# Attention over 16 heads of width 16: one block of keys in four as one full-width product, and stores waited for by halves

## The reference

```python
rx = _apply_rope(x)
q, k, v = (proj(Wq, bq), proj(Wk, bk), proj(Wv, bv))     # 16 heads of width 16
scores = jnp.einsum('bhqd,bhkd->bhqk', q, k) / np.sqrt(hd)
attn = jax.nn.softmax(scores, axis=-1)
attended = jnp.einsum('bhqk,bhkd->bhqd', attn, v)
attended = attended.transpose(0, 2, 1, 3).reshape(b, s, d)
return attended @ Wo.T + bo
```

## Time and profile before

| | us |
|---|---|
| median of 3 runs | 2109.47 (2102.84 to 2113.85) |
| the profiled execution | 2103.16 |
| its span in the profile | 2101.8 |
| TensorE busy in the span | 1683.6 (80%) |
| VectorE busy | 1234.1 (59%) |
| ScalarE busy | 1032.3 (49%) |
| POOL busy | 988.7 (47%) |

### The profile page before, as it was taken

The page is one execution under the profiler, slowest core; times in us unless marked ns, Lnnn a source line. Parts: engine busy times, 40 slices in busy tenths (PEclk is TensorE's granted clock), DMA queues, the critical chain, the costliest instruction groups (busy, mean ns, idle before and its releaser), DMA issues. The chain is left out here.

```text
span 2101.8 us, 23811 instructions
## 1 busy us (share of the span) xinstructions
PE 1683.6 (80%) x7418; PEld 1232.8 (59%) x7419; DVE 1234.1 (59%) x2317; ACT 1032.3 (49%) x1981; POOL 988.7 (47%) x824
## 2 busy tenths in 40 slices
PE   5698894999935887878882989989998998679882
PEld 2477673777723665656652656656666665556661
DVE  5655554666547685959853665575675674452224
ACT  2154442555401675757782665665675765052220
POOL 1200002243233474657770574574674676048884
PEclk9899997999965898999996999999999999669996
DMA  2300003444235222213002010120120110138776
GB/s 78 122 11 31 1 21 126 114 126 111 61 85 130 71 61 62 50 46 85 21 1 98 21 42 21 32 61 21 31 60 24 29 52 24 59 77 200 179 178 161
DMA packets 96787, 146.17 MB, mean 70 GB/s; under 512 B 22711, under 2 KB 61820, under 8 KB 93830
## 3 DMA queue, kind: packets, MB, share of 16 engines
q1 hardware_dynamic: 65104, 102.69, 16.9%
q0 software_dynamic: 18432, 26.36, 6.9%
q10 hardware_dynamic: 13126, 15.60, 2.4%
HBM read 101.83 MB, written 36.41 MB: 66 GB/s over the span
## 5 line engine op out<-in xcount | busy, mean ns | idle before, releaser
L2183 POOL TENSOR_TENSOR STp_lo_use<-ST_use,STp_hi_use 128x512 fp32r<-128x512 f32 x256 | 333.8, 1312 | 227.8 <-ACT ST_use L2032 226.7
L1712 POOL TENSOR_TENSOR STp_lo<-ST,STp_hi 128x512 fp32r<-128x512 f32 x192 | 255.8, 1349 | 141.1 <-ACT ST L1480 140.3
L2096 DVE TENSOR_REDUCE nmax_use<-bank 128x1 f32<-128x512 f32 x256 | 173.3, 679 | 114.4 <-PE bank L1940 110.0
L2028 ACT ACTIVATE STp_hi_use<-bank 128x512 fp32r<-128x512 f32 x256 | 153.0, 597 | 173.2 <-PE bank L1966 170.4
L1476 ACT ACTIVATE STp_hi<-bank 128x512 fp32r<-128x512 f32 x256 | 158.8, 620 | 82.2 <-PE bank L1414 81.5
L1601 DVE TENSOR_REDUCE nmax<-bank 128x1 f32<-128x512 f32 x256 | 168.6, 680 | 41.5 <-PE bank L1403 41.0
L1403 PE MATMUL bank<-rows_k,rows_q 65*128 65x512 f32 x256 | 125.4, 498 | 66.0 <-DVE nmax L1601 48.1
L1480 ACT ACTIVATE ST<-bank 128x512 f32<-128x512 f32 x256 | 160.0, 625 | 0.0
L2032 ACT ACTIVATE ST_use<-bank 128x512 f32<-128x512 f32 x256 | 151.8, 593 | 2.1 <-POOL STp_lo_use L2183 2.1
L1940 PE MATMUL bank<-ks,qs 128*128 128x512 f32 x256 | 112.2, 440 | 36.2 <-DVE nmax_use L2096 14.9
L918 POOL TENSOR_SCALAR veps<-mv 128x4 f32<-128x4 f32 x4 | 0.9, 228 | 249.6 <-DVE mv L867 249.6
(11 more groups left out here) (428 smaller groups left out, 4558.6 us busy)
## 6 DMA issues: line engine op xcount, KB each, us to landing
stage<-in_W SPq DMA_DIRECT2D x16, 1024.0 KB, 4.9
Wgu<-in_Wgu SPq DMA_DIRECT2D x32, 384.0 KB, 3.4
rows_q<-hop_scratch SPq DMA_DIRECT2D x32, 256.0 KB, 4.6
ks<-ks SPq DMA_DIRECT2D x64, 128.0 KB, 2.3
rinv<-rinv_scratch SPq DMA_DIRECT2D x64, 128.0 KB, 2.9
rows_k<-hop_scratch SPq DMA_DIRECT2D x24, 256.0 KB, 5.6
hop_scratch<-qkp_hi SPq DMA_DIRECT2D x20, 256.0 KB
Wda<-in_Wdn SPq DMA_DIRECT2D x32, 128.0 KB, 3.6
```

Source lines behind the costliest of these rows:

```text
L1712: G.tensor_tensor(STp[u % NHI][1], ST[u % NFULL], plain(STp[u % NHI][0]), ALU.subtract).then_inc(low["pool"].sem, low["pool"].inc(u))
L2028: A.activation(STp[u % NHI][0], bk.ap, ACT.Exp)
L2096: V.tensor_reduce(nmax[:, (h % 2) * TB + j:(h % 2) * TB + j + 1], bk.ap, AX.X, ALU.max, negate=True).then_inc(bk.free, 1)
L2183: G.tensor_tensor(STp[u % NHI][1], ST[u % NFULL], plain(STp[u % NHI][0]), ALU.subtract).then_inc(low["pool"].sem, low["pool"].inc(u))
```

## The change

One block in four, u % 4 = 3, is called whole. For it ScalarE takes the exponential once, in full, into one of two new buffers `whole_ST`; there is no subtraction; and TensorE weighs it in one full-width float32 product with the same stationary columns. The other three blocks stay as they were, all their subtractions on POOL. The pairs of `STp` become four, used by these blocks alone, and the buffers `ST` three.

SP's stores of q's and k's parts wait for the first half, issue its stores, and then wait for the second half. ScalarE, before it writes a half of `qkp`, waits for the stores of that half alone. Stores of q stand at step 30 of the program where they were at 33, stores of k at 36 where they were at 39; no other issue of SP lies between. VectorE waits for its own last division before the next one.

```diff
-    NHI, NFULL = 5, 4
+    NHI, NFULL = 4, TB - 1
+        whole_ST = [sb("whole_ST%d" % z, [P, S]) for z in range(2)]
-        low_by = [("dve" if u % 4 == 3 else "pool") for u in range(END)]
+        whole = [u % TB == TB - 1 for u in range(END)]
+        low = Signal(kit, "s4_low", [u for u in range(END) if not whole[u]])
+        def parts_of(u):
+            return STp[(u // TB * NFULL + u % TB) % NHI]
...
-                    PE.wait_ge(low[low_by[u]].sem, low[low_by[u]][u])
-                    PE.matmul(bk.ap, Vone[:, kt, h, :], STp[u % NHI][0], start=k == 0 and kt == 0, stop=False)
-                    PE.matmul(bk.ap, Vone[:, kt, h, :], STp[u % NHI][1], start=False, stop=k == HG - 1 and kt == TB - 1).then_inc(weighed.sem, weighed.inc(u))
+                    if whole[u]:
+                        PE.wait_ge(ST_BANKS[u % 2].free, ST_BANKS[u % 2].free_at["scores", u])
+                        PE.matmul(bk.ap, plain(Vone[:, kt, h, :]), whole_ST[u // TB % 2], start=False, stop=k == HG - 1).then_inc(weighed.sem, weighed.inc(u))
+                    else:
+                        PE.wait_ge(low.sem, low[u])
+                        PE.matmul(bk.ap, Vone[:, kt, h, :], parts_of(u)[0], start=k == 0 and kt == 0, stop=False)
+                        PE.matmul(bk.ap, Vone[:, kt, h, :], parts_of(u)[1], start=False, stop=False).then_inc(weighed.sem, weighed.inc(u))
...
+                    if whole[u]:
+                        if u >= 2 * TB:
+                            A.wait_ge(weighed.sem, weighed[u - 2 * TB])
+                        A.activation(whole_ST[u // TB % 2], bk.ap, ACT.Exp).then_inc(bk.free, 1)
...
-                            all_hopped(A, b if n else b - 1, 1 - n)
+                            A.wait_ge(hopped[1 - n][g].sem, hopped[1 - n][g][b if n else b - 1, len(HOPS[1 - n]) - 1])
...
-                if 0 <= u < END and low_by[u] == "dve":
-                    bk = ST_BANKS[u % 2]
-                    V.wait_ge(bk.free, bk.free_at["scores", u])
-                    if u >= NHI:
-                        V.wait_ge(weighed.sem, weighed[u - NHI])
-                    V.tensor_tensor(STp[u % NHI][1], ST[u % NFULL], plain(STp[u % NHI][0]), ALU.subtract).then_inc(low["dve"].sem, low["dve"].inc(u))
...
+                        if b or g:
+                            V.wait_ge(att_done.sem, att_done[(b, g - 1) if g else (b - 1, GROUPS - 1)])
...
-                    b = of_next(s, (33, 39)[n])
+                    b = of_next(s, (30, 36)[n])
                     if b:
-                        for g in range(DC):
-                            SP.wait_ge(stack_bank(b, n, g).free, stack_bank(b, n, g).free_at["stack", b, n, g])
                         if b > 1 and n == 0:
                             for i in range(QUARTERS):
                                 SP.wait_ge(stacked[i].sem, stacked[i][b - 2, 3])
                         for g in range(DC):
+                            SP.wait_ge(stack_bank(b, n, g).free, stack_bank(b, n, g).free_at["stack", b, n, g])
                             hop(SP, b, n, g)
```

More of the change, by code:

```diff
@@ L1282, in self_heads @@
         v_zeroed = Signal(kit, "s4_v_zeroed", ["V"])
-        low_by = [("dve" if u % 4 == 3 else "pool") for u in range(END)]
-        low = {e: Signal(kit, "s4_low_" + e, [u for u in range(END) if low_by[u] == e]) for e in ("dve", "pool")}
+        whole = [u % TB == TB - 1 for u in range(END)]
+        low = Signal(kit, "s4_low", [u for u in range(END) if not whole[u]])
         rowed = [Signal(kit, "rowed%d" % z, [(b, i) for b in range(B) for i in range(z, QUARTERS, 2)], step=16) for z in range(2)]
@@ L1310, in head_columns, with parts_free @@
             return bass.AP(Vone.tensor, Vone.offset + g * HG * P + n, [Vone.ap[0], [H1 * P, TB], [P + BLOCK, HG], [1, k]])
+        def parts_of(u):
+            return STp[(u // TB * NFULL + u % TB) % NHI]
+        def parts_free(u):
+            n = u // TB * NFULL + u % TB - NHI
+            return n // NFULL * TB + n % NFULL if n >= 0 else None
         def of_batch(s, r):
@@ L1706, in pool @@
                 u = s - ST_LAG - 1
-                if 0 <= u < END and low_by[u] == "pool":
+                if 0 <= u < END and not whole[u]:
                     bk = ST_BANKS[u % 2]
                     G.wait_ge(bk.free, bk.free_at["scores", u])
-                    if u >= NHI:
-                        G.wait_ge(weighed.sem, weighed[u - NHI])
-                    G.tensor_tensor(STp[u % NHI][1], ST[u % NFULL], plain(STp[u % NHI][0]), ALU.subtract).then_inc(low["pool"].sem, low["pool"].inc(u))
+                    before = parts_free(u)
+                    if before is not None:
+                        G.wait_ge(weighed.sem, weighed[before])
+                    G.tensor_tensor(parts_of(u)[1], ST[u % TB], plain(parts_of(u)[0]), ALU.subtract).then_inc(low.sem, low.inc(u))
                 for c in range(DC):
```

16 lines of the change are left out of this document (8 added, 8 removed).

## The result

| | before | after |
|---|---|---|
| median (range) of 4 runs each, us | 2106.15 (2102.48 to 2113.85) | 2056.74 (2050.18 to 2063.77) |
| ratio, 95% interval | | 0.976 (0.9736 to 0.9785) |
| span of the profiled execution | 2101.8 | 2048.9 |
| granted clock over the span | 0.908 | 0.915 |

The forecast was 2077 us with 2056 to 2102 as its range: right in direction, 20 us too high, and the time lies at the range's low edge.

The account below looks back on a forecast made before the run. VectorE was taken as late, in small pieces everywhere and large ones at batch boundaries. Terms -17 - 13.5 - 2 + 0 = -32.5 us; against the timed median of 2109.5 the forecast is 2077 us, range 2056 to 2102.

Parts of the forecast that it names:

- Halves: Batch boundaries: storing and waiting by halves removes ScalarE's three DMA waits and some slow clock; -17 us (-8 to -19).
- what would show it: Signs of right: no DMA wait before L1521, first-half stores within 1 us, plain stretches 35 to 37 us, VectorE under 32.
- Plain stretches: Three stretches of plain running: VectorE's subtraction goes, TensorE sets the pace; -13.5 us (-20 to -3).
- The floor of 34.4 us: Plain stretch of 32 steps: TensorE's own work after the change, 31.2 + 8 x 0.40 us.
- Price of the full-width product: TensorE, each whole block: 0.86 us against 0.46 for the fp32r pair, +0.40 us, 64 times 25.6 us.
- Boundaries: First 32 blocks of each batch: whole blocks' dearer products and removed subtractions cancel; 0 us (-8 to +8).
- 1013.8 to 1061.5 and the end: End of batch 2: -2 us, waits go; last 33 us: 0 us, POOL full before and after.
- TensorE eats the relief: Rival, plain stretches: dearer product cancels the relief, only the halves' gain remains; 2092 us, chance 0.14.
- The halves bring nothing: Rival, boundaries: ScalarE waits for stores as before, only the whole blocks' gain remains; 2094 us, chance 0.08.
- Slower: Rival: full product on the path everywhere, no relief from VectorE; +12 us, 2121 us, chance 0.05.
- The pauses take the clock with them: Rival: boundaries run at full clock and win 5 us each beyond the sum; 2060 us, chance 0.07.

Follow-up runs that it names:

- e1: Kernel before with only SP's stores and ScalarE's waits done by halves, no whole blocks; 2084.20 us, ratio 0.9899.
- e7: Changed kernel, but ScalarE again waits for the stores of both halves while SP still issues them by halves; 2067.32 us, ratio 0.9784.
- e2: Changed kernel with SP's stores and ScalarE's waits as before, so only one block in four whole; 2075.57 us, ratio 0.9857.
- e3: Kernel before without VectorE's 64 subtractions, ScalarE's second exponential written as the low part, TensorE's product pair kept; 2078.67 us, ratio 0.9876.
- e8: Changed kernel run once more, word for word, for a second trace; 2057.35 us, ratio 0.9746.
- e6: Changed kernel with two blocks in four whole instead of one, 128 full-width products; 2071.98 us, ratio 0.9823.
- e5: Changed kernel with each whole block weighed by two fp32r products (0.46 us) instead of one full-width product (0.86); 2047.58 us, ratio 0.9701.

## Why the prediction was right in direction and too small

**Halves: mechanism right, size 2.7 us short.** Forecast -17 (to -19), e1 gives -19.7 at the boundaries. No DMA wait is left before L1541, and the stores go out within 1 us, as "what would show it" asked. That the sum came so near is in part luck: its part for the clock was scaled from the second boundary to all three, and e1 took 12.2, 4.9 and 2.7 us off the three. The longest landing of a store, 7.8 us, was misread: by line, the 3.0 to 7.8 us of the earlier trace rows are those of the 20 loads (L1582), and the profile gives none for the stores (L1571). The conclusion held; the last of q's stores was issued at 807.18 us and ScalarE released by 813.89, 6.7 us later. Which of the two edits does it was not asked (e7).

**Plain stretches: right.** Forecast -13.5, measured -13.8, and -14.3 in the second trace. VectorE is under 32.1 us in each. The floor of 34.4 us was 0.6 short: the third stretch takes 35.0 with no gap. The others, at 39.2 and 39.7, took longer than the 35 to 37 that the text named; they began at 43.8 and 44.4 by this cut, so the gain was there and the level was not.

**Price of the full-width product: right.** It was taken from two rows of other shapes. TensorE's timeline in the changed kernel, the scores' product of three steps, the first step with a whole block:

```profile
944.96 0.40 PE L1425 MATMUL bank<-rows_q,rows_k 66*128 66x512 f32 x1
...
946.29 0.40 PE L1425 MATMUL bank<-rows_q,rows_k 66*128 66x512 f32 x1
...
947.23 0.40 PE L1425 MATMUL bank<-rows_q,rows_k 66*128 66x512 f32 x1
```

1.33 us against 0.94: +0.39, forecast +0.40.

**Boundaries: the step that failed.** The prediction gave the whole blocks 0 us here (between -8 and +8): "24 products add 9.6 us and up to 4 us more at the lower clock; 24 subtractions go, but a good half of them lie in time in which VectorE waits for ScalarE anyway". Measured -10.5 alone (e2). The subtractions were sized about right: the text left them some 10 to 13 us to cancel the products, and e3, which removes them alone, gives 11.0 (193.0 against 204.0). What failed is the charge on the other side, 9.6 us in full and up to 4 us more at the lower clock: with it e2 would lie 9.6 to 13.6 us above e3, and it ends at 193.5 us against 193.0. Two things stand in its place. At one and the same granted clock the price reaches the end in part: 2.1 of 3.2 us in the second boundary (64.8 us in e3 and 66.9 in e2, both at 0.92), and 5.4 to 5.9 of 9.6 us over the three, between e5 and the changed kernel. The error there was to charge TensorE's work in full at a place where it had idle time (55.22 us busy in a second boundary of 69.4), one paragraph after writing that "what counts is the place". And the clock moved the other way: instead of a surcharge at the lower level, it stands at 0.87, 0.92 and 0.92 with the whole blocks alone, where the kernel before has 0.81, 0.86 and 0.90 and e3 0.81, 0.92 and 0.88. How the rest divides between this clock and the 24 exponentials that e2 saves and e3 does not is open; no run takes the exponentials away alone.

**1013.8 to 1061.5 and the end: right.** Forecast -2 and 0; measured -0.3 and -1.6 in the first trace, -2.8 and -1.6 in the second. The last stretch takes 30.2 us where the same cut has 31.8 before; on the 33.0 of the earlier trace rows that is some 31.4, just under the 32 to 34 of the text. The Trainium skill (SBUF — State Buffer, section "SBUF: two separate sides") has the loser of the port pair that VectorE and GpSimd share blocked for a whole instruction, and by that rule the end would be 1 to 2 us shorter; the trace agrees with its POOL part (1349 to 1314 ns a subtraction; VectorE's own took 0.68 us in the median, 1.02 in the mean and 1.78 at most), but e3 shows that this alone doesn't shorten the stretch (31.6 us, ScalarE the bound): it took the saved exponential as well.

**The sum.** With the terms as e1 and e2 have them, the boundaries give -30.2 instead of -17, and the stage -45.7; measured -43.2 and -45.8. The medians differ by 49.4 us here and 53.3 beside e8. What stands between 45 and 50 to 53 us is not settled: the profiled execution of the kernel before has a higher granted clock (0.908) than the seven that were timed beside e8 (0.900 to 0.907), so its time lies low, and the intervals of the ratios are 5 to 8 us to either side.

**The rivals.** *TensorE eats the relief* and *The halves bring nothing* fall with e1 and e2. *Slower* falls with e6: even with 128 full-width products the kernel is 1.8% faster than before. *The pauses take the clock with them* is near the truth in its size (2060), and partly in its mechanism: the granted clock of the first two boundaries went from 0.81 and 0.86 to 0.92 and 0.95, the third from 0.90 to 0.95. But in e3 the first boundary is 3.6 us shorter at the same 0.81, so the clock is not its one cause; how much of the 27.5 us is clock was not separated.

## What to carry to other kernels

Charge a dearer instruction in full only where its engine has no idle time: the same 0.40 us cost 1.5 us per four in the stretch without gaps, a little over half to two thirds of its sum in the boundaries, and nothing in the two plain stretches where TensorE would otherwise wait for VectorE. Price it with a run that changes nothing else (e5 against e8); runs that lighten another engine at the same time (e6, or e2 against e3) made the boundaries look free. When a wait is long on an engine's row, ask whether the engine is late or early: VectorE's 25.8 us behind ScalarE were worth nothing when removed, TensorE's 11.5 us behind a bank were worth 12 to 13. A bank whose next user stands in the same step as a producer with two followers costs their whole chain; one step of distance or another bank gave it back here.

## What the runs showed of the hardware

The granted clock at the start of a boundary falls to its lower level in the kernel before and in the changed one alike. Busy time of the changed kernel in pieces of 4 us:

```profile
768.00:772.00 4.00, 3.25 (x11) 1.55 (x9) 3.42 (x4) 1.85 (x5) 4.00 (x3) 1.00 0.95 182
772.00:776.00 4.00, 1.20 (x4) 0.68 (x4) 3.19 (x4) 2.25 (x6) 3.89 (x3) 1.00 0.00 0
776.00:780.00 4.00, 2.90 (x7) 2.35 (x8) 3.69 (x6) 2.46 (x5) 1.75 (x2) 0.53 0.00 0
780.00:784.00 4.00, 4.00 (x14) 2.85 (x13) 1.35 (x3) 1.77 (x3) 1.01 (x2) 0.62 0.00 0
```

TensorE was idle 2.00 and 2.15 us there, waiting for maxima that VectorE took only behind steps of the rope, and in the 8 us behind them the granted clock is 0.53 and 0.62, mostly the lower level (0.50, 1.2 GHz). In the kernel before it fell a second time behind the idle 4.84 us of the earlier trace rows, where eight products took 3.78 us instead of 1.99; that second fall is gone in the changed one. The idle gaps of 1.56 us in the changed kernel were not followed by one.
